# Two of four chunks of a mixture-of-experts layer sorted by expert instead of by expert group

## What is computed

```
logits = xf @ router_weight.T                       # 16 experts, in 4 groups of 4
scores = sigmoid(logits); s_choice = scores + router_bias
group_scores = top_k(s_choice by group, 2)[0].sum(-1)
keep the 2 best groups, mask the others; topk_idx = top_k(masked, 4)
w = scores[topk_idx]; w = w / (w.sum(-1) + 1e-20) * 2.5
out = sum over the 4 chosen e of w_e * ((silu(xf @ w_gate[e].T) * (xf @ w_up[e].T)) @ w_down[e].T)
```

## Time and profile before

| | us |
|---|---|
| median of 3 runs | 1984.54 (1981.78 to 1986.18) |
| profiled execution | 1974.37 |
| its span | 1972.6 |

### The profile page before, as it was taken

The page is one execution under the profiler, slowest core; times in us unless marked ns, Lnnn a source line. Parts: engine busy times, 40 slices in busy tenths (PEclk is TensorE's granted clock), DMA queues, the critical chain, the costliest instruction groups (busy, mean ns, idle before and its releaser), DMA issues. The chain is left out here.

```text
span 1972.6 us, 40622 instructions
## 1 busy us (share of the span) xinstructions
PE 1605.6 (81%) x15110; PEld 1419.5 (72%) x15110; DVE 1054.6 (53%) x2359; ACT 748.8 (38%) x1301; POOL 503.7 (26%) x437
## 2 busy tenths in 40 slices
PE   7979999999998764687627899887686887988974
PEld 6868888888887764676625676676576887977974
DVE  5636644655456533445446777775453364436442
ACT  5334344434444311253314766763122232332321
POOL 4054121112200044433442333331322203024031
PEclk9999999999999867797867989996597998989987
DMA  6236442133200321364420000004421222123222
GB/s 238 89 99 200 133 132 95 65 112 130 92 18 2 128 86 64 117 190 132 148 88 5 1 2 1 0 1 172 158 76 65 71 77 79 56 66 107 70 76 71
DMA packets 105922, 173.36 MB, mean 88 GB/s; under 512 B 11168, under 2 KB 78880, under 8 KB 104864
## 3 DMA queue, kind: packets, MB, share of 16 engines
q1 hardware_dynamic: 89296, 130.04, 19.6%
q0 software_dynamic: 14016, 40.39, 6.4%
q10 hardware_dynamic: 2448, 0.61, 0.2%
HBM read 87.51 MB, written 83.49 MB: 87 GB/s over the span
## 5 line engine op out<-in xcount | busy, mean ns | idle before, releaser
L115 PE MATMUL e_p_gu<-e_w_hi,e_xt_hi 128*128 (+1 forms) x868 | 267.2, 308 | 42.8 <-DVE e_xt_lo L701 30.4
L115 PE MATMUL e_p_gu<-e_w_hi,e_xt_lo 128*128 (+1 forms) x868 | 260.2, 300 | 7.3 <-issue 7.0
L115 PE MATMUL e_p_gu<-e_w_lo,e_xt_hi 128*128 (+1 forms) x868 | 260.2, 300 | 6.1 <-issue 5.8
L1318 DVE SCALAR_TENSOR_TENSOR e_gated<-e_gated,e_share,e_p_gu 128x128 f32<-128x128 f32 x320 | 96.9, 345 | 232.2 <-ACT e_gated L1242 207.0
L115 PEld LDWEIGHTS e_p_gu<-e_w_hi,e_xt_hi 128*128 128x128 f32 x868 | 181.5, 209 | 44.2 <-issue 42.4
L115 PEld LDWEIGHTS e_p_gu<-e_w_hi,e_xt_lo 128*128 128x128 f32 x868 | 181.1, 209 | 10.1 <-issue 10.0
L115 PEld LDWEIGHTS e_p_gu<-e_w_lo,e_xt_hi 128*128 128x128 f32 x868 | 181.8, 209 | 7.7 <-issue 7.7
L1242 ACT ACTIVATE e_gated<-e_p_gu 128x256 f32<-128x256 f32 x160 | 61.2, 384 | 287.7 <-PE e_p_gu L115 219.2
L115 PE MATMUL e_p_y<-e_w_hi,e_hid_hi 128*128 (+1 forms) x434 | 148.3, 342 | 6.3 <-issue 6.0
L1218 POOL DMA_INDIRECT e_xn<-results,e_row_of x64 | 64.8, 1012 | 314.8 <-issue 211.0
L115 PE MATMUL e_p_y<-e_w_lo,e_hid_hi 128*128 (+1 forms) x434 | 128.5, 296 | 2.0 <-issue 2.0
(11 more groups left out here) (332 smaller groups left out, 4422.6 us busy)
## 6 DMA issues: line engine op xcount, KB each, us to landing
results<-e_y SPq DMA_DIRECT2D x81, 256.0 KB
e_moved<-rows SPq DMA_DIRECT2D x40, 272.0 KB, 2.8
pa_x<-in_x SPq DMA_DIRECT2D x7, 1536.0 KB, 6.3
e_moved<-rows SPq DMA_DIRECT2D x41, 256.0 KB
w_qk_in<-in_we SPq DMA_DIRECT2D x24, 384.0 KB, 6.3
we_parts<-w_qk_in SPq DMA_DIRECT2D x24, 384.0 KB, 2.3
we_parts<-a_e_lo SPq DMA_DIRECT2D x24, 384.0 KB, 2.4
rows<-a_zero SPq DMA_DIRECT2D x8, 1088.0 KB, 5.9
```

What stands on the lines that cost most here:

```text
L115: mm = eng.matmul(out, lhs[a], rhs[b], start=start and n == 0, stop=stop and n == len(terms) - 1, skip_group_check=skip)
L1318: last = dve.scalar_tensor_tensor(gated[h % 2][:, b, :], gated[h % 2][:, b, :], share[x % 2][:, b, j:j + 1], up[:, b, :], ALU.mult, ALU.mult)
```

## The change

`grouped_phase` becomes `sorted_phase`, which takes a `Sorting` for each chunk. Chunks 0 and 3 stay sorted by group. Chunks 1 and 2 are sorted by expert:

- 16 lists, each row in four of them: four scatters and four gathers for each block. The room is 64 and 48 sorted blocks (32 and 24 pairs), each with one expert, so a sorted pair is one unit. Rows are 256 wide, as the weights don't travel; they are applied in the combine, which is then four dependent operations for one block. A ring buffer holds one block's four results.
- Routing of these chunks sums over the 16 lists (up to 12 x 16 columns instead of 12 x 4), finds the expert of each of up to 64 blocks, and picks the four weights of each row. For chunk 1 eight of its pieces are done in one step; a step with an own pair first finishes what is pending.
- The own pairs of chunk 2 stand in chunk 0 and those of chunk 3 in chunk 1, two each behind the fifth and the sixth sorted pair. Scatter 2 comes ahead of gather 0 and scatter 3 ahead of gather 1 in GpSimd's queue.
- The steps of the combines follow a table (`combine1`).
- The row and result buffers in DRAM of chunks 1 and 2 grow, and so what the first attention stage zeroes.

The core of the diff:

```diff
-MOVES = (("scatter", 0), ("scatter", 1), ("gather", 0), ("scatter", 2), ("gather", 1), ("scatter", 3), ("gather", 2), ("gather", 3))
+MOVES = (("scatter", 0), ("scatter", 1), ("scatter", 2), ("gather", 0), ("scatter", 3), ("gather", 1), ("gather", 2), ("gather", 3))
...
+@dataclass
+class Sorting:
+
+    lists: int
+    members: int
+    k: int
+    entry: int
+
+    def rooms(self, chunk):
+        return most_blocks((chunk[1] - chunk[0]) * P, self.k, self.lists)
+
+    def width(self):
+        return ROW if self.members > 1 else D
+
+
+BY_GROUP, BY_EXPERT = Sorting(GROUPS, E1 // GROUPS, GROUP_K, 2), Sorting(E1, 1, 4, 1)
+SORTED = (BY_GROUP, BY_EXPERT, BY_EXPERT, BY_GROUP)
...
     def __init__(self, chunks, rooms, members):
+
         own = lambda c: [("own", c, j) for j in range((chunks[c][1] - chunks[c][0]) // 2)]
         self.order = own(0) + own(1)
         for c in range(len(chunks)):
-            late = own(c + 1) if 1 <= c < len(chunks) - 1 else []
+            late = own(c + 2) if c + 2 < len(chunks) else []
             for j in range(rooms[c] // 2):
-                self.order += [("sorted", c, j)] + late[2 * j:2 * j + 2]
+                self.order += [("sorted", c, j)]
+                if j >= 4:
+                    self.order += late[2 * (j - 4):2 * (j - 4) + 2]
...
-        self.turn_at = [-1 if i < 2 else self.first_unit[i - 1] + 1 if not self.is_own[i - 1] else self.last_unit[i - 2]
+        self.turn_at = [-1 if i < 2 else self.first_unit[i - 1] + 1 if self.last_unit[i - 1] > self.first_unit[i - 1] else self.last_unit[i - 2]
...
+    rooms = [by.rooms(chunk) for by, chunk in zip(sorting, chunks)]
+    flow = Flow(chunks, rooms, [by.members for by in sorting])
+    total = len(flow.units) + 3
+    entries = [(c, first) for c, (low, high) in enumerate(chunks) for first in range(low, high, sorting[c].entry)]
...
+        yg = [xn[:, top_k * i:top_k * (i + 1), 0:D] for i in range(RING)]
...
+        burst = [99, 8] + [0] * (len(chunks) - 2)
+        chosen_in = [6 if by.members > 1 else 10 + math.ceil(n / 6) for by, n in zip(sorting, counts)]
...
-            combine_at[g] = flow.chunk_end[c] + 7 + math.ceil(2.3 * ((first - chunks[c][0]) // 2 + 1))
+        for g, (c, first) in enumerate(entries):
+            combine_at[g] = flow.chunk_end[c] + combine_step(c, (first - chunks[c][0]) // sorting[c].entry)
...
-                    sp.wait_ge(picked, x - LOADS + 1)
-                sp.dma_start(moved[x % LOADS][:], d["rows"][c][2 * P * j:2 * P * (j + 1)].rearrange("(b p) n -> p b n", p=P))\
+                    at_least(sp, picked, picks[x - LOADS + 1])
+                sp.dma_start(moved[x % LOADS][:, :, 0:sorting[c].width()], d["rows"][c][2 * P * j:2 * P * (j + 1)].rearrange("(b p) n -> p b n", p=P))\
                     .then_inc(loaded[x % LOADS], 16)
...
                 for n in range(*chunks[c]):
-                    for k in range(GROUP_K):
+                    for k in range(sorting[c].k):
                         pool.indirect_dma_start(out=d["rows"][c][0:rooms[c] * P],
                                                 out_offset=bass.IndirectOffsetOnAxis(ap=row_of[:, n, k:k + 1], axis=0),
-                                                in_=own_rows(n), in_offset=None, bounds_check=rooms[c] * P - 1,
+                                                in_=own_rows(n)[:, 0:sorting[c].width()], in_offset=None, bounds_check=rooms[c] * P - 1,
                                                 oob_is_err=False).then_inc(scattered[c], 16)
...
+                    for n in range(sorting[c].entry):
+                        for k in range(sorting[c].k):
+                            pool.indirect_dma_start(out=yg[g % RING][:, k * sorting[c].entry + n, :], out_offset=None,
                                                     in_=d["results"][c][0:rooms[c] * P],
                                                     in_offset=bass.IndirectOffsetOnAxis(ap=row_of[:, first + n, k:k + 1], axis=0),
...
+                if flow.order[i][1] in single:
+                    dve.tensor_tensor(gated[h % 2][:], gated[h % 2][:], up, ALU.mult).then_inc(valued, 1)
+                    return
...
+                if not by_group:
+                    dve.tensor_copy(of_list(sel_bf_, c), sel.rearrange("p b e -> p e b")).then_inc(sel_ready, 1)
+                then(dve.tensor_tensor(comb, sel, scores, ALU.mult))
                 yield
...
+                    for n in range(count):
+                        last = dve.max(top[:, n, :], placed[:, n, :])
+                    then(last)
+                    ends = top[:, :, 0:top_k]
+                dve.tensor_scalar(row_of[:, low:high, 0:by.k], ends, -1.0, None, ALU.add).then_inc(routed, 1)
...
+                    far = work[0:1, 0:rooms[c] * lists].rearrange("p (j e) -> p j e", e=lists)
+                    upto = cum[0:1].rearrange("p (j e) -> p j e", j=1).broadcast_to([1, rooms[c], lists])
+                    here = core.steps[0:1, 0:rooms[c]].rearrange("p (j e) -> p j e", e=1).broadcast_to([1, rooms[c], lists])
...
+                which = work[:, 0:count * top_k * experts].rearrange("p (b k e) -> p b k e", k=top_k, e=experts)
+                per_choice = lambda a: a.rearrange("p b (k e) -> p b k e", k=1).broadcast_to([P, count, top_k, experts])
+                mine = top[:, :, 0:top_k].rearrange("p b (k e) -> p b k e", e=1).broadcast_to([P, count, top_k, experts])
+                then(dve.tensor_tensor(which, per_choice(placed), mine, ALU.is_equal))
+                yield
+                then(dve.tensor_tensor(which, which, per_choice(comb), ALU.mult))
+                yield
+                then(dve.tensor_reduce(weight[:, low:high, :], which, AX.X, ALU.add))
+                then(dve.tensor_scalar(weight[:, low:high, :], weight[:, low:high, :], 2.5, None, ALU.mult))
...
             def combine(g):
 
-                _, first = groups[g]
-                rows = core.h[:, first:first + 2, :]
-                dve.wait_ge(gathered[g % RING], 16 * 2 * GROUP_K * (g // RING + 1))
-                dve.tensor_tensor(rows, rows, yg[g % RING][:, 0], ALU.add).then_inc(halfway, 1)
-                dve.wait_ge(halfway, g + 1)
-                dve.tensor_tensor(rows, rows, yg[g % RING][:, 1], ALU.add).then_inc(combined, 1)
+                c, first = entries[g]
+                by, got = sorting[c], yg[g % RING]
+                dve.wait_ge(gathered[g % RING], 16 * top_k * (g // RING + 1))
+                rows = core.h[:, first:first + by.entry, :]
+                for k in range(by.k):
+                    if k > 0:
+                        dve.wait_ge(halfway, rounds[g] + k)
+                    if by.members > 1:
+                        last = dve.tensor_tensor(rows, rows, got[:, 2 * k:2 * k + 2, :], ALU.add)
+                    else:
+                        last = dve.scalar_tensor_tensor(rows[:, 0, :], got[:, k, :], weight[:, first, k:k + 1], rows[:, 0, :], ALU.mult, ALU.add)
+                    last.then_inc(combined if k == by.k - 1 else halfway, 1)
...
+                    if pending is not None:
+                        for _ in pending:
+                            pass
                     take_logits(flow.units[s][0])
...
-                        if c == 0:
-                            for _ in pending:
-                                pass
+                        for _ in range(burst[c]):
+                            next(pending, None)
...
-                    if s == flow.last_unit[flow.last_own[c]] + (0 if c == 0 else 9):
+                    if s == flow.last_unit[flow.last_own[c]] + (0 if c == 0 else max(0, chosen_in[c] - burst[c]) + 1):
                         count_rows(c)
...
+def combine1(c, entry):
+
+    wait, apart = ((13, 1.9), (6, 1.9), (7, 2.2), (7, 2.2))[c]
+    return wait + math.ceil(apart * (entry + 1))
...
-    rooms = [most_blocks((high - low) * P, GROUP_K, GROUPS) * P for low, high in CHUNKS]
-    dram["rows"] = [nc.dram_tensor(f"rows{c}", (rows, ROW), F32).ap() for c, rows in enumerate(rooms)]
+    rooms = [by.rooms(chunk) * P for by, chunk in zip(SORTED, CHUNKS)]
+    dram["rows"] = [nc.dram_tensor(f"rows{c}", (rows, SORTED[c].width()), F32).ap() for c, rows in enumerate(rooms)]
```

More of the change, by code:

```diff
@@ L1206, in gather @@
                 if c == 0:
-                    for sent in range(sum(low < CH + 2 * GROUP_K * RING for low, _ in chunks)):
-                        pool.wait_ge(scattered[sent], 16 * counts[sent] * GROUP_K)
+                    for sent in range(sum(low < CH + top_k * RING for low, _ in chunks)):
+                        pool.wait_ge(scattered[sent], 16 * counts[sent] * sorting[sent].k)
                 for i in range(STORES):
                     pool.wait_ge(y_stored[i], 16 * sum(x % STORES == i for x in range(flow.moves_in[c])))
-                for g, (of, first) in enumerate(groups):
+                for g, (of, first) in enumerate(entries):
                     if of != c:
@@ L1267, in _ @@
                     hidden_high(s - 1)
```

(3 more changed lines are left out.)

191 lines of the change are left out of this document (105 added, 86 removed).

## The result

The changed kernel takes **2148.57 us** (median of 4 runs, 2146.96 to 2152.57) where the kernel before takes 1985.36 (4 runs, 1981.78 to 1989.63): a ratio of **1.0824 [1.0798, 1.0851]**. It is slower by 163 us and lies outside the range, on the side to which the prediction gave 0.35.

A forecast was written before the change was run, and what follows sets the result against it. The second expert layer was taken as bound by TensorE's own work plus what it loses while GpSimd issues indirect DMAs. Terms -71.7 + 58.2 + 4 = -9.5 us gave a median of 1975 us, range 1938 to 2012.

The forecast's parts named there:

- Part 1: Second expert layer, chunks 1 and 2: 24 grouped pairs become 56 single pairs of 3.18 us each, -71.7 us.
- Part 3: Order of scatters and logits two chunks ahead, in GpSimd's and SyncE's queues: waits hidden, own pairs only move, 0 us.
- Part 2: GpSimd's 80 more scatters and gathers in the second layer stall TensorE by a law of burst length: +58.2 us.
- Rival 4: No loss by DMAs at all, the stalls having a cause that doesn't grow: 1917 us, chance 0.06.
- Part 4: VectorE's combines and routing in the second layer: hidden in the mean, bounds 0 and 12, taken as +4 us.
- Rival 2: Single pairs paced by VectorE: +18, 1993 us, chance 0.12; sign: a pair over 3.3 us without any DMA of GpSimd.
- Part 5: Zero fills of larger row buffers, spread over the attention stage: 7 more, hidden, 0; without cover at most 41 us.
- the fours running together: Gathers 1 and 2: 60 DMAs come so close they cost as in a burst of 12: +45, 2020 us, chance 0.18.
- the size of bursts: Long bursts of GpSimd's DMAs cost less, 0.8 us for each DMA: -32, 1943 us, chance 0.12.

The follow-up runs named there:

- e6: Changed kernel with all four chunks sorted by group as before, so only the order of scatters and logits is new: 1801.89 us, ratio 0.9989 to the kernel before.
- e7_by_due_step: Changed kernel with SyncE's loads, stores and outputs sorted by the step at which each is due: 1736.95 us against 1803.71 for the kernel before.
- e8: Kernel before with every scatter of the second layer followed by a second one into a buffer nobody reads: 2064.42 us against 1972.95, ratio 1.0466.
- e1: Changed kernel with SyncE's stores issued three pairs later in its queue: 1753.05 us against 1801.13 for the kernel before, ratio 0.9725.
- e7: Runs on a faster chip: changed kernel with SyncE's queue by due step, without and with GpSimd's DMAs spread, 1736.95 and 1734.29 us, against the kernel before, 1803.71.
- e7_before: Kernel before, unchanged, run for its trace on a faster chip: 1805.03 us in one run.
- e5_after_again: Changed kernel, unchanged, run again on a faster chip: 1930.48 us against 1803.52 for the kernel before, ratio 1.0713.
- e8_store_behind: Changed kernel with SyncE's store of a pair issued three pairs later, on a chip where bursts cost time: 1977.05 us in one run against 1972.95.
- e3: Kernel before with the 64 indirect scatters of the second layer as plain DMAs on the same queue: 1800.42 us in one run against 1801.13.

## Why the prediction was wrong

**Part 1 failed, in "3.18 us each, with their loads, stores and register loads".** The 3.18 of the earlier trace rows is the pace of the first layer, whose loop issues the store three pairs later. The second layer's has `store(x)` straight ahead of `load(x + 5)`. I carried the duration over with its loads and never asked in which order they stand. The 56 single pairs were put at 178 us; 48 of them took 349. With the store moved, these 48 took 187 on the last chip, 33 of them by the terms for its bursts: the size of a single pair was right, and what was missing was the loop around it.

**Part 3 was right, on the first chip, in what it claims, and blind where it should have looked.** The order and the early logits cost nothing that can be told (e6, on a chip of the other kind). That the combines of chunk 0 don't wait it took from TensorE standing still in a burst. In the kernel after they don't; on a chip without the stall one of them waits 4.1 us (e7_by_due_step). But of SyncE it asks only whether the load of chunk 2 waits for scatter 2. The wait that decided is no new one: a load behind a store, which in the kernel before had 10.4 us a turn. It could be worked out: 0.46 us from store to load in the two couples of the kernel before, 2.7 us to landing (the median of its loads in the same stretch), and behind it the turn, the down products and the copy. The first two alone are 3.16, the whole of the 3.18, before the engines' part is added.

**Part 2 was right on the first chip, and a law of that kind of chip alone.** In the kernel after, the burst of 48, in the timelines of GpSimd and ScalarE:

```profile
1454.57 0.98 POOL L1238 DMA_INDIRECT rows<-e_xn,e_row_of  x1 [36.38 <-DVE e_row_of L1479]
...
1515.68 0.99 POOL L1238 DMA_INDIRECT rows<-e_xn,e_row_of  x1 [0.30 <-issue]
```

```profile
1455.29 0.38 ACT L1280 ACTIVATE e_gated<-e_p_gu 128x256 f32<-128x256 f32 x1 [1.78 <-PE e_p_gu L135]
...
1527.41 0.38 ACT L1280 ACTIVATE e_gated<-e_p_gu 128x256 f32<-128x256 f32 x1 [2.79 <-PE e_p_gu L135]
```

72.1 us for five units, 13.0 due: 59.1 lost, predicted 57.8. e8 gives 59.2 in another kernel, and 56.7 (1438.55 to 1508.27) in the changed one. On the chips of e1 to e7 the term is near nothing. Rival 4, no loss by DMAs, had -67.7 us; e7_by_due_step, the change with its loop taken away on such a chip, has 1736.95 - 1803.71 = -66.8. By the Trainium skill ("SBUF — State Buffer", "SBUF: two separate sides") a DMA and a compute engine don't slow each other: e7_before agrees, with 0.8 us lost in a burst of 24, and the first chip and the last don't, with 28 and 59 us. What the page speaks of are the ports of SBUF; whether the stall has to do with them no run tells.

**Part 4**: VectorE is hidden, 3.19 us a pair with combines (e7_by_due_step): 0 and not +4, apart from the one combine named above. Rival 2's sign did appear in the kernel after (over 3.3 us with GpSimd silent), but VectorE was busy for 10.93 of 50 us there. A sign that two mechanisms share names neither.

**Part 5**: hidden, as far as can be told. ScalarE's gates of the first layer by their line (count, ns min/median/max, first and last start) in e7_before, e5_after_again, the kernel before and the kernel after:

```profile
L645 ACT ACTIVATE e_gated<-e_p_gu x57: 384/384/387, 660.4 to 908.6; 128x256 f32<-128x256 f32 x57
...
L665 ACT ACTIVATE e_gated<-e_p_gu x57: 383/383/385, 660.5 to 908.6; 128x256 f32<-128x256 f32 x57
...
L645 ACT ACTIVATE e_gated<-e_p_gu x57: 383/383/432, 661.2 to 996.1; 128x256 f32<-128x256 f32 x57
...
L665 ACT ACTIVATE e_gated<-e_p_gu x57: 383/383/432, 666.7 to 1006.4; 128x256 f32<-128x256 f32 x57
```

On the quicker kind of chip the fills cost 0.1 us by then; on the first chip the first gate comes 5.5 us later in the kernel after, of which one trace of each can't say whether it is the fills or the spread of single executions (the kernel before spreads over 8 us there).

**The rivals** had the fours running together, VectorE, and the size of bursts, and none had SyncE's queue. The right mechanism was outside the list, so its chance was not too small but missing. The sum itself, -9.5 us, stands beside +4 us for e8_store_behind, which is the change with its loop taken away: one run, where the kernel before spreads over 19 us, so the two aren't told apart.

## What to carry to other kernels

The duration of a step is only worth what the order of the queues around it makes of it: before a pace is carried from one stage to another, write down for each DMA queue what stands ahead of each load, and follow that back to the load before. Where a change makes a step shorter, compare every loop of waits (issue, landing, engines, store, next issue) with the new length, those above all that cost nothing at the old one. And a store should stand neither so early that a load behind it waits for a result, nor behind a load that itself waits long, as for a scatter, while the result's buffer is missed: sorting the queue by due steps gave both.

## What was not expected of the hardware

Chips of one type differ by what GpSimd's indirect DMAs do to the engines. The kernel before takes 1985.36 and 1972.95 us on two chips and 1801 to 1804 on three. A burst of 24 lost 28.0 us on the first and 0.8 us on a chip of the other kind, and one of 48 lost 57 to 59 us on both chips of the first kind. Of the 182 us between the first chip and e7's, 174 lie between the first and the last gate of the two expert layers (334.9 and 248.2 us by the rows at part 5, 523.1 and 435.7 in the second), the stages with the indirect DMAs. In the stall the engines show no data to wait for: of the kernel after's burst of 48, the 41.7 us before one gate are put down to "remote", some 2.4 us before each of several matmuls to "issue". The transposes of the earlier trace rows are put down to VectorE, which was busy for 5.28 of 35 us. What stops them, and why on some chips only, is open. e3 was meant to separate the indirect descriptors from the transfer and ran on a chip without the stall; no run here tells them apart.
